# Attention over image rows: turns of one key tile, and every product on halves of the rows of the array

## The reference

```
q = Wq h;  k = Wk h;  v = Wv h          # 8 heads of 64 channels
attn = softmax(q^T k)  over the 2304 keys, per head
out  = attn v;  sc = Wsc h
result = x + gamma * out + sc
```

## Time and profile before

| | before |
|---|---|
| time, median of 3 runs | 3122.99 us (3122.82 to 3123.27) |
| profiled execution, first to last instruction | 3120.7 us |
| PE busy | 3078.5 us, 99% |
| POOL busy | 2787.6 us, 89% |
| DVE busy | 2284.6 us, 73% |
| ACT busy | 2244.3 us, 72% |
| granted TensorE clock | 0.998 |

### The profile page before, as it was taken

How to read it: one execution, slowest core, us unless ns; L and a number is a source line. 1 busy time by engine, 2 the same in 40 slices (tenths; PEclk the granted TensorE clock), 3 DMA queues, 4 the chain that set the end, 5 groups by cost and what they waited for, 6 DMA issues and landing times.

```text
span 3120.7 us, 119616 instructions
## 1 busy us (share of the span) xinstructions
PE 3078.5 (99%) x52307; PEld 2183.3 (70%) x52307; DVE 2284.6 (73%) x3624; ACT 2244.3 (72%) x4020; POOL 2787.6 (89%) x2039
## 2 busy tenths in 40 slices
PE   6999999999999999999999999999999999999998
PEld 4677777767777677777777777777776777767766
DVE  7777777777787777777777777777777777777774
ACT  5676787777676777777667677778776767667676
POOL 1788999999898899999889899999988989889899
PEclk9999999999999999999999999999999999999999
DMA  3111110110112011110112111111101010101011
GB/s 130 31 40 39 30 47 23 45 34 23 36 40 59 20 38 41 27 53 25 24 33 57 40 29 41 38 31 46 23 25 24 22 27 20 29 20 28 21 29 30
DMA packets 168968, 110.78 MB, mean 35 GB/s; under 512 B 120320, under 2 KB 166400, under 8 KB 168448
## 3 DMA queue, kind: packets, MB, share of 16 engines
q1 hardware_dynamic: 168448, 103.13, 12.6%
HBM read 56.10 MB, written 18.87 MB: 24 GB/s over the span
## 4 chain that ended last, share of the span: by engine, by line
PE 91%; POOL 5%; ACT 0%; issue 0%; DVE 0%; ACTq 0%; DVEq 0%
PE SL L441 25%; PE PJ L380 19%; PE MX L413 11%; PE OB L465 10%; PE OB L462 9%; PE OB L464 9%; PE PJ L377 6%; POOL PLO L954 5%; PE SL L436 1%; ACT PE L558 0%; POOL half L950 0%; ACT L676 0%; DVE mx L753 0%; DVE PLO L923 0%; PE SL L389 0%
## 5 line engine op out<-in xcount | busy, mean ns | idle before, releaser
L954 POOL TENSOR_TENSOR PLO<-PE 128x768 f16<-128x768 f32 x1727 | 2551.0, 1500 | 266.8 <-ACT PE L558 255.5
L558 ACT ACTIVATE PE<-SL 128x768 f32<-128x768 f32 x1728 | 1307.3, 809 | 27.6 <-PE SL L441 27.5
L462 PE MATMUL OB<-V,PE 128*128 128x65 f16 x10368 | 1048.5, 193 | 6.8 <-POOL PLO L954 5.7
L464 PE MATMUL OB<-V,PE 128*128 128x64 f16 x10368 | 1048.5, 193 | 0.0
L465 PE MATMUL OB<-V,PLO 128*128 128x65 f16 x10368 | 1048.2, 196 | 0.0
L462 PEld LDWEIGHTS OB<-V,PE 128*128 128x128 bf16 x10368 | 965.1, 99 | 58.2 <-POOL PLO L954 11.7
L441 PE MATMUL SL<-QK 64*128 64x384 f16 x10368 | 1000.8, 323 | 0.1
L464 PEld LDWEIGHTS OB<-V,PE 128*128 128x128 bf16 x10368 | 962.5, 97 | 42.9
L566 ACT ACTIVATE MXC<-MX 128x384 f32<-128x384 f32 x864 | 423.3, 490 | 752.2 <-PE MX L413 752.2
L465 PEld LDWEIGHTS OB<-V,PLO 128*128 128x128 f16 x10368 | 963.4, 98 | 0.0
L753 DVE TENSOR_REDUCE mx<-MX 128x2 f32<-128x768 f32 x864 | 828.4, 959 | 84.4 <-PE MX L413 38.0
(11 more groups left out here) (105 smaller groups left out, 1237.9 us busy)
## 6 DMA issues: line engine op xcount, KB each, us to landing
gx<-x SPq DMA_DIRECT2D x36, 768.0 KB, 4.7
xr<-x SPq DMA_DIRECT2D x96, 192.0 KB, 2.4
out<-xr SPq DMA_DIRECT2D x96, 192.0 KB, 1.9
X<-x SPq DMA_DIRECT2D x6, 768.0 KB, 8.5
CR<-c SPq DMA_TRANSPOSE x96, 2.4
back<-half SPq DMA_TRANSPOSE x95, 2.8
QK<-wk SPq DMA_DIRECT2D x1, 1024.0 KB, 12.7
QK<-wv SPq DMA_DIRECT2D x1, 1024.0 KB, 13.4
```

What stands on the lines that cost most here:

```text
L462: pe.matmul(acc, upper, v[:, D:V1], start=k == 0 and h == 0 and i == 0, stop=False, skip_group_check=True)
L464: pe.matmul(acc[:, 0:D], upper, v[:, 0:D], start=False, stop=False, skip_group_check=True)
L558: act.activation(PE32[:, s % PB, :].rearrange("p (h n) -> p h n", h=2), SL[s % 2][:, :, 0:CH], ACT.Exp, scale=1.0 / SS).then_inc(s_exp, 1)
L954: nc.gpsimd.tensor_tensor(PLO[:, s % PB, :], PE32[:, s % PB, :], PE32[:, s % PB, :].bitcast(BF16)[:, 1:4 * CH:2], ALU.subtract).then_inc(s ...
```

## The change

- A turn is one key tile. PE does `score(s)`, the first half of `weigh(s - 3)`, `top`, the slots of the projections, and the second half of `weigh` (at the four starts of a block of slots and at k = 2, that half stands ahead of the slots). `LAG` = 3: weighing is three steps behind.
- `weigh` is done in two parts. Each product of 128 rows becomes two of 64 rows. In part 0 the rows 0 to 63 take one head and rows 64 to 127 the other, in part 1 they are swapped. `OB` is two banks, one per head. Part 1 waits for part 0 (`s_half`).
- Projections are on halves of the rows too: in a block of slots the lower half of the rows of one unit is done beside the upper half of the unit before it, in the two banks of `PJ`. The upper half waits for the lower (`s_low`).
- `SL` is one pair of banks, and the differences of keys are to one tile back (`KF` has 128 columns of zeros ahead, before 256). `score(s)` waits for `exp(s - 1)`, before for `exp(s - 2)`. The shift is put in at k = 0 only.
- `top` is taken out by one DVE maximum of 768 for every tile; ACT's copy and DVE's maximum of the copy are gone.
- The upper part of the keys of a later block is made from `KF` (`keys_upper`, L597) in the step behind `leave`; `DF` has two buffers.

```diff
@@ PE, main loop @@
             for n in range(CHUNKS):
-                for m in range(DS):
-                    s = n * MT + 2 * m
+                for k in range(MT):
+                    s = n * MT + k
                     U = s + LEAD
+                    b, lo, hi = block_of(k)
+                    score(n, k)
+                    if s >= LAG:
+                        weigh(s - LAG, 0)
                     if U < TOPS:
                         top(U)
-                    score(n, 2 * m)
-                    score(n, 2 * m + 1)
-                    if U < TOPS:
-                        top(U + 1)
-                    u = slot_unit(n, m)
-                    if u:
-                        project(u, *sixths(n, m))
-                    if s:
-                        weigh(s - 2)
-                        weigh(s - 1)
+                    if s >= LAG and (lo == 0 or k == 2):
+                        weigh(s - LAG, 1)
+                    for i in range(lo, hi):
+                        slot(4 * n + b, i)
+                    if s >= LAG and not (lo == 0 or k == 2):
+                        weigh(s - LAG, 1)
@@ the slots of a chunk @@
+STARTS = (0, 4, 9, 13)
+SLOTS = (3, 3, 3, 3, 3, 2, 3, 2, 2, 3, 3, 3, 3, 3, 2, 3, 2, 2)
@@ PSUM @@
-        SLS = ctx.enter_context(nc.psum_tensor("SL", [P, 4, 512], F32))
-        SL = [SLS[:, 2 * i:2 * i + 2, :] for i in range(2)]
+        SL = ctx.enter_context(nc.psum_tensor("SL", [P, 2, 512], F32))
         MX = ctx.enter_context(nc.psum_tensor("MX", [P, 2, 512], F32))
-        OB = ctx.enter_context(nc.psum_tensor("OB", [P, 512], F32))
-        PJ = ctx.enter_context(nc.psum_tensor("PJ", [P, 512], F32))
+        OB = ctx.enter_context(nc.psum_tensor("OB", [P, 2, 512], F32))
+        PJ = ctx.enter_context(nc.psum_tensor("PJ", [P, 2, 512], F32))
@@ PE, a slot of the projections @@
+            def slot(J, i):
+                begun, ended = unit_in(J), unit_in(J - 1)
+                if begun and i == 0:
+                    left(same_bank_before(begun))
...
+                if ended and i == 0:
+                    pe.wait_ge(s_low, PLACE[ended] - OPENING + 1)
...
+                for a in range(QT):
+                    if a < low:
+                        one = term(begun, slice(0, D), i, a)
...
+                    if a < high:
+                        one = term(ended, slice(D, P), i, a)
@@ PE, score @@
-                if s >= 2:
-                    pe.wait_ge(s_exp, s - 1)
+                if s:
+                    pe.wait_ge(s_exp, s)
@@ PE, weigh(s, part) @@
+                else:
+                    pe.wait_ge(s_half, s + 1)
+                cross = (s + part) % 2
+                for i in range(QT):
+                    for piece in range(3):
+                        for half_rows in range(2):
+                            r = slice(half_rows * D, (half_rows + 1) * D)
+                            h = half_rows ^ cross
...
+                            acc = OB[:, h, i * OW:i * OW + AW]
+                            v = V[r, g % 2, k, h * V1:(h + 1) * V1]
@@ ACT @@
-            def top_copy(U):
...
-                act.activation(MXC[:, :], MX[:, 1, 0:CH], ACT.Copy).then_inc(s_mxc, 1)
@@ DVE @@
-            def top_other(U):
...
-                nc.vector.tensor_reduce(mx3[:, n % 2, 1, k:k + 1], MXC[:, :], AX.X, ALU.max).then_inc(s_mxr, 1)
@@ DVE, main loop @@
-                    if m in (3, 5) and n >= 2:
-                        add_result(n - 2, m // 2 - 1)
+                    if k in (6, 10) and n >= 2:
+                        add_result(n - 2, (6, 10).index(k))
```

More of the change, by code:

```diff
@@ L41 @@
 LEAD = MT + 4
+LAG = 3
 KH, DH, DL, QH, QL = range(5)
@@ L56, with block_of, unit_in, done_at @@
 BY_SCALAR = (0, 3)
-def slot_unit(n, m):
+STARTS = (0, 4, 9, 13)
+SLOTS = (3, 3, 3, 3, 3, 2, 3, 2, 2, 3, 3, 3, 3, 3, 2, 3, 2, 2)
+TERMS = 3 * CT
+def block_of(k):
+    b = max(i for i, at in enumerate(STARTS) if at <= k)
+    lo = sum(SLOTS[STARTS[b]:k])
+    return b, lo, lo + SLOTS[k]
+def unit_in(J):
+    if J < 0 or J >= 4 * CHUNKS:
+        return None
+    n, b = divmod(J, 4)
+    if b == 0:
+        return ("sc", n)
     if n >= LAST:
-        return ("sc", n) if m < 6 else None
-    if m < 3:
-        return ("sc", n)
+        return None
     g, c = divmod(n, NCH)
-    kind, part = AHEAD[3 * c + (m - 3) // 2]
+    kind, part = AHEAD[3 * c + b - 1]
     return (kind, g + 1, part)
[L70 to L81, removed]
-        return None
-    n, m = divmod(M, DS)
-    u = slot_unit(n, m)
-    return u if u and sixths(n, m)[1] == 6 else None
-def root_unit(n, m):
+def done_at(s):
+    if s < 0:
+        return None
+    n, k = divmod(s, MT)
+    if k + 1 != MT and k + 1 not in STARTS:
+        return None
+    return unit_in(4 * n + block_of(k)[0] - 1)
+def root_unit(n, k):
     g, c = divmod(n, NCH)
-    if m == DS - 1 and g % PAIRS == 1 and g // PAIRS + 1 < BATCH and c < 2:
+    if k == MT - 1 and g % PAIRS == 1 and g // PAIRS + 1 < BATCH and c < 2:
         return ("r", g // PAIRS + 1, c)
@@ L98, in units @@
     out = [(kind, 0, c) for kind, c in FIRST + BESIDE]
-    for n in range(CHUNKS):
-        out += [done_at(n * DS + m) for m in range(DS) if done_at(n * DS + m)]
+    out += [unit_in(J) for J in range(4 * CHUNKS) if unit_in(J)]
     out.append(("f", CHUNKS - 1))
@@ L210, in build @@
         s_rest = sem("s_rest")
+        s_half = sem("s_half")
         s_av = sem("s_av")
@@ L262, in norm_piece, with norm_part @@
             return (g % PAIRS - 1) * (NCH // 2) + c - NCH // 2
-        def norm_part(n, m, late):
+        def norm_part(n, k, turns):
             g, c = divmod(n, NCH)
-            if norm_piece(n) is None or not 0 <= m - late < CT:
+            if norm_piece(n) is None or k not in turns:
                 return None
-            return (g // PAIRS, norm_piece(n), m - late)
+            return (g // PAIRS, norm_piece(n), turns.index(k))
         @block.sync
@@ L382, in project, with term @@
                 if hi == 6:
                     last.then_inc(s_pj, 1)
-            def root(b, part):
+            def term(u, rows, i, a):
+                kind, dst = u[0], bank(u)
+                g, c = divmod(u[1], NCH) if kind == "sc" else u[1:]
+                b, j = divmod(g, PAIRS)
+                t, (wp, p) = i // 3, PARTS3[i % 3]
+                edge = dict(start=rows.start == 0 and i == 0 and a == 0, skip_group_check=True,
+                            stop=rows.start > 0 and i == TERMS - 1)
+                if kind == "v":
+                    m = c * QT + a
+                    return pe.matmul(dst[:, a * P:(a + 1) * P], X[rows, b % 2, p, t, m * P:(m + 1) * P],
+                                     WT[rows, 2, wp, t, j * P:(j + 1) * P], **edge)
+                return pe.matmul(dst[:, 0:CH], WT[rows, WEIGHT[kind], wp, t, j * P:(j + 1) * P],
+                                 X[rows, b % 2, p, t, c * CH:(c + 1) * CH], **edge)
@@ L467, in weigh @@
-                last.then_inc(s_av, 1)
+                if part == 0:
+                    if k == 0:
+                        if n:
+                            pe.wait_ge(s_oe, n)
+                        left(("v", g, NCH - 1))
+                    if s + 1 < STEPS:
+                        pe.wait_ge(s_rest, s + 1)
+                    else:
+                        pe.wait_ge(s_restd, 1)
+                else:
+                    pe.wait_ge(s_half, s + 1)
+                cross = (s + part) % 2
@@ L470, in _ @@
+                last.then_inc(s_half if part == 0 else s_av, 1)
             pe.wait_ge(s_const, 3)
```

317 lines of the change are left out of this document (144 added, 173 removed).

## The result

| | before | changed |
|---|---|---|
| time, median | 3123.05 us (4 runs) | 3081.66 us (3080.0 to 3082.9, 4 runs) |
| ratio | | **0.9867** [0.9853, 0.9881] |
| profiled execution, span | 3120.7 us | 3078.3 us |
| a chunk, mean over 90 | 31.81 us | 31.17 us |

The changed kernel is 1.3% faster. The forecast was 2.8%: right in direction and inside the stated range (2965 to 3230 us), but less than half of the gain came.

A forecast was written before the change was run, and what follows sets the result against it. PE's own instruction stream was taken as the bound. Opening 86.9 + 90 chunks of 30.64 (2757.6) + last six chunks and tail 184.7 + norms 3 = 3032 us, with 2.3 from span to median 3034; range 2965 to 3230 us.

The forecast's parts named there:

- PE's own stream sets the time, and the change of rows costs 0.10 us: On PE, switching between all rows and halves loses 0.10 us, twice a turn; removing nine turns' switches saves 1.80 us a chunk.
- Rival C: The 0.10 us comes from a PSUM bank change or semaphore, not the row switch: 3207 us; chance 0.05.
- Short pairs cost what one full product did: In `weigh`, a pair of half-row products takes 0.0306 us, the same as one full product.
- Rival A: Short pairs in `weigh` cost more than one product: gain gone at 0.0335 us, 3986 us at the upper bound; chance 0.15.
- The chain through SL takes 1.57 us: From `score(s)` through ACT's exp to `score(s+1)`: 1.57 us, hidden in three-slot steps, costing 0.24 us a chunk in two-slot ones.
- Rival B: The chain through SL binds every step because exp comes later: break-even 1.75 us a step, 3210 us at 1.80; chance 0.15.
- POOL hides: POOL needs 29.0 us a chunk, under 30.64, with about two steps of slack: costed at nothing, next in line.
- Bank of the projections: Projection slots waiting for a unit to be taken out: hidden with 0.1 us to spare, 0.1 us a chunk taken.
- `add_result` on DVE: DVE's add takes 1.24 us and delays the maximum, making `top` late by 0.17 and 0.05 us: 0.2 us a chunk.
- `s_half`: Part 1 of `weigh` waits for part 0 where it follows `top` directly: five steps, 0.05 us each, 0.25 a chunk.
- array work and chain (the base of the sum): Array work left per chunk, 31.81 less 1.96 = 29.85 us, plus 0.24 us for the chain through SL.
- the "+ 3 for the three later norms": 3 us in the whole run for the later norms' small full-row products behind a wait for DVE.

The follow-up runs named there:

- Experiment 6: Changed kernel with only the projections, or only weighing, back on all 128 rows: 3352.1 us (ratio 1.0735) and 3672.16 us (1.1758).
- experiment 1: Changed kernel with the two result additions per chunk left out, a one-column copy in their place: 3040.35 us, ratio 0.9734.
- experiment 7: Changed kernel with halves not swapped in weighing: 3063.19 us; separately, with the later norms' square root replaced by a copy: 3074.16 us.
- experiment 8: Changed kernel with 6 or 18 more PE instructions per step, from waits met long before, no array work: 3369.79 us and 4658.52 us.

## Why the prediction was right or wrong, point by point

**What was right.**
- *PE's own stream sets the time, and the change of rows costs 0.10 us.* Experiment 6: 0.104 us in one kernel, 0.2 us for two in the other. Rival C fell: banks change at every one of these places in the changed kernel too, and it loses nothing there.
- *Short pairs cost what one full product did.* 0.031 us a pair, two products and two loads. Rival A fell. The 25 ns that the prediction quoted from the Trainium skill ("TensorE: Matmul & The Clock Gate") do not bind between the halves: two starts came in 31 ns, 36 products in 0.55 us.
- *The chain through SL takes 1.57 us.* Steps of two slots took 1.56 to 1.57 where nothing else stood in them; PE's waits name ACT's exp five times in the whole run. Rival B fell.
- *POOL hides.* No wait of PE names it. Yet it cost time through DVE's add, which I did not have.
- *Bank of the projections:* no row of waits for it. Steps 4, 9 and 13, which wait for the bank and for `s_half`, last 1.772 to 1.780 us, and step 2, which waits for `s_half` alone, 1.773.

**What was wrong: terms of the sum that were mis-sized.** The span came out 46 us over the 3032.

| step of the prediction | forecast | measured | over 90 chunks |
|---|---|---|---|
| **`add_result` on DVE** | 0.2 us a chunk | 0.59 (k = 8: 0.35, k = 12: 0.24) | +35 us |
| **`s_half`** and the waits for the banks | 0.25 + 0.1 | 5 x 0.083 | +6 us |
| array work and chain (the base of the sum) | 29.85 + 0.24 | 29.90 | -17 us |
| single steps (the "+ 3 for the three later norms") | 3 us | 24.5 us | +22 us |
| opening, last six chunks and tail | 271.6 us | 273.0 | +1 us |

1. *`add_result`.* The step that failed is "takes 1.24 us". The row gives the time from start to end as a constant of the instruction. It was the rest of POOL's split, 0.83 us, plus 0.41. In the new order the add meets POOL earlier in its split and takes 1.45, 0.21 more, twice a chunk; `top` came 0.18 us later than forecast at k = 8 and 0.19 at k = 12. The rest of the arithmetic of that step held. With the add gone, the time fell by 41 us (experiment 1), nearly the size of the whole miss; but 11 us of its 52 went into other losses. That POOL is next in line was in the prediction; that DVE's add waits for it was not.
2. *Single losses.* Of the 24.5 us, by steps: k = 17 of six chunks (6, 7, 30, 31, 54, 55), in the stretches of the later norms, 6 x 0.97 = 5.8 us; the table loads, 3 x 2.14 = 6.4 us (experiment 7: 7.5 us came back); a step at the lower clock in chunk 56, 1.3 us; the seven gaps without a wait 4.2 us (experiment 8). Some 6.8 us are spread over smaller delays and stay unnamed. The prediction's 3 us were for the small products of the norms alone, and those stand in the steps of the 5.8. The table loads it put at nothing without a word, though before there was a second pair of banks for SL to hide them; and the instruction supply was "part of rival A", by a price per pair and not as a stall of its own.
3. *`s_half`.* 0.083 instead of 0.05 a place, which nothing in the trace of before could show.
4. *The base, an error that helped.* 29.85 was taken from the mean chunk before. The prediction's own step prices give 12 x 1.694 + 6 x 1.531 + 0.163 = 29.68, 0.17 less, and that with the chain's 0.24 is what was measured (29.90). About half of the 0.17 are rare waits of the kernel before (its typical chunk is 31.73 us, its mean 31.81), which were then counted again; the rest stays open. With the right base the forecast would have been 15 us lower and the miss some 61 us, so that the total came as near as it did is in part luck.

No rival came true; more than half of the gain forecast was lost in waits that were given too little (the add) or no place at all (the table loads, the gaps).

## What to carry to other kernels

An instruction's length in a profile is not its cost when another engine shares its port: compare its end with the end of the other engine's instruction before you move it, and if the difference is constant, count that and the rest of the other's instruction. And leave the other engine pauses there: without them the instruction can be passed over. When a change takes the slack out of the bounding engine (here: switches, a second pair of banks), cost again every rare event that the slack had hidden, the table loads among them. And when products are halved, count instructions as well as array time: each pair was free here, but the stream came, as experiment 8 is read here, within a few per cent of the pace at which instructions arrive.

## What the runs showed of the hardware that was not expected

- An add from SBUF to SBUF on DVE ends 0.413 to 0.416 us behind the end of a GpSimd instruction (5th to 95th percentile of 190; the two that met no GpSimd instruction took 0.61 and 0.62 from start to end). GpSimd's next one is delayed in turn where it follows without a pause (1.78 us instead of 1.47). Six GpSimd instructions without a pause held one add for 5.32 us, three of them passing it over; in the kernel before none was passed over. With one input it is 0.213 to 0.217 us, and it waits all the same.
- PE stands still with nothing to wait for, 2.3 to 2.8 us behind the start of a transfer of instructions: 7 gaps with one transfer in 4.2 us, 315 with 6% more instructions (4.36 us), one or none at 5.0 and above. Late instructions are the likely cause, not a shown one.
- A wait that has long been met, as an instruction of its own, cost 28 ns with 6 in a step (288 us / 10362), most of it in the gaps, and 51 ns with 18 (1577 us / 31086), where there were no gaps.
- After the stop of 1.94 us in chunk 56 the mean granted clock of the next 5 us was 0.66, so two thirds of them stood at the lower of its two levels (1.2 GHz); in chunk 32, over 5 us that begin 0.5 us behind the end of a stop of the same length, it was 1.00. The windows of both (window, length, busy time and instructions of PE, PEld, DVE, ACT and POOL, then the clock, here 0.66 and 1.00):

```profile
1839.50:1844.50 5.00, 5.00 (x105) 4.05 (x107) 1.92 (x3) 2.45 (x4) 4.53 (x4) 0.66 0.02 3
1092.00:1097.00 5.00, 5.00 (x162) 4.22 (x160) 3.48 (x6) 3.88 (x7) 5.00 (x5) 1.00 0.01 3
```
